# Twelve activation turns of the second pass by DMA transposes instead of TensorE, with the lists of ScalarE and VectorE reordered

## The reference, cut to what matters

```python
# first branch, "d" is a long convolution of the context, worked out apart
y  = layernorm(layernorm(x));  y = silu(y @ W1a + b1a) @ W1b + b1b + ...   # first pass
y  = y * d                                                                 # gate
z  = layernorm(y) * g2 + be2;  z = silu(z @ W2a + b2a) @ W2b + b2b + y     # second pass
x  = x + tanh(g_xattn) * z
# second branch: experts on heads of 32 numbers
h  = layernorm(x) @ Wm + bm                    # "third norm" and "head products"
t  = h.reshape(-1, 32);  w = softmax(t @ expert_emb);  top-2 of 16 experts
x  = x + tanh(g_ffn) * (sum of two experts of t, weighted) @ Wo + ...
```

## Time and profile before

| | |
|---|---|
| runs | 808.10, 813.09, 814.97 us; median 813.09 us |
| span of the profiled execution | 807.5 us |
| PE busy | 774.8 us (96%) |
| ACT busy | 670.3 us (83%) |
| DVE busy | 531.4 us (66%) |
| POOL busy | 496.0 us (61%) |
| second pass | about 180 to 300 us from the start |
| experts | from about 300 us to the end |

### The profile page before, as it was taken

One profiled execution on the slowest core, in us unless ns is written; L12 is line 12 of the kernel. 1 busy time (PEld: TensorE's weight loads), 2 busy tenths in 40 slices (PEclk: granted clock), 3 DMA queues, 4 the chain that ended last, 5 costly groups with the idle time before them and its releaser, 6 DMA issues.

```text
span 807.5 us, 23892 instructions
## 1 busy us (share of the span) xinstructions
PE 774.8 (96%) x9972; PEld 380.7 (47%) x9972; DVE 531.4 (66%) x988; ACT 670.3 (83%) x840; POOL 496.0 (61%) x389
## 2 busy tenths in 40 slices
PE   9999788889999998998999999999999999999997
PEld 4667455646676664333334434434434433434433
DVE  5999854557688985684665664764764764664445
ACT  4465854445869878799999999999999999999995
POOL 1374332027753542585787787787787787787674
PEclk9999999979999999999999999999999999999999
DMA  8990699941133316655465554555555555465552
GB/s 291 219 244 28 135 187 191 198 107 36 50 86 89 89 44 166 156 143 149 145 158 151 166 157 147 159 170 146 157 159 151 165 159 155 148 171 158 149 154 67
DMA packets 85971, 117.06 MB, mean 145 GB/s; under 512 B 13123, under 2 KB 65475, under 8 KB 85764
## 3 DMA queue, kind: packets, MB, share of 16 engines
q1 hardware_dynamic: 85864, 115.55, 55.2%
HBM read 101.28 MB, written 6.94 MB: 134 GB/s over the span
## 4 chain that ended last, share of the span: by engine, by line
PE 71%; DVE 10%; ACT 7%; SPq 5%; issue 3%; DMA 2%; POOL 2%; POOLq 0%; DVEq 0%; ACTq 0%
PE PB L792 26%; PE PA L780 18%; PE PT L780 9%; PE PA L581 5%; SPq L345 4%; PE PB L598 3%; PE PB L814 2%; PE PA L535 2%; DMA RA<-wpd 2%; DVE WK L897 2%; DVE SM L914 1%; ACT WK L1458 1%; PE PT L673 1%; ACT WK L1438 1%; ACT WK L1435 1%
## 5 line engine op out<-in xcount | busy, mean ns | idle before, releaser
L1677 POOL TENSOR_TENSOR WK<-WK 128x512 f32<-128x512 f32 x238 | 320.3, 1346 | 112.3 <-DVE WK L1333 102.2
L1582 ACT ACTIVATE WK<-PA 128x1024 f32<-128x1024 f32 x349 | 360.1, 1140 | 10.8 <-PE PA L780 10.3
L792 PE MATMUL PB<-WK,EW 128*32 128x512 f32 x2040 | 264.7, 594 | 0.4 <-DVE WK L1333 0.4
L780 PE MATMUL PA<-RA,EW 98*32 98x512 f16 x2800 | 201.6, 380 | 0.5 <-ACT WK L1582 0.5
L1582 ACT ACTIVATE WK<-PT 128x1024 f32<-128x1024 f32 x163 | 187.1, 1148 | 2.0 <-PE PT L780 1.7
L1610 POOL TENSOR_TENSOR WK<-WK 128x512 f16<-128x512 f32 x64 | 79.5, 1255 | 129.9 <-ACT WK L1438 128.6
L780 PEld LDWEIGHTS PA<-RA,EW 98*32 98x32 f16 x2800 | 68.1, 95 | 154.9 <-issue 80.4
L780 PE MATMUL PT<-RA,EW 98*32 98x512 f16 (+1 forms) x1312 | 99.6, 379 | 4.8 <-ACT WK L1582 3.4
L792 PEld LDWEIGHTS PB<-WK,EW 128*32 128x32 f32 x2040 | 62.4, 111 | 52.3 <-DVE WK L1333 0.9
L1333 DVE SCALAR_TENSOR_TENSOR WK<-PB,CV,W2h 128x512 f32<-128x512 f32 x64 | 48.1, 751 | 49.1 <-PE PB L792 49.1
L1333 DVE SCALAR_TENSOR_TENSOR WK<-PB,CV,W2l 128x512 f32<-128x512 f32 x63 | 47.3, 751 | 44.3 <-PE PB L792 44.3
(11 more groups left out here) (220 smaller groups left out, 1086.8 us busy)
## 6 DMA issues: line engine op xcount, KB each, us to landing
RA<-wpd SPq DMA_DIRECT2D x128, 134.1 KB, 5.8
W1h<-wtd SPq DMA_DIRECT2D x128, 128.0 KB, 2.7
DC<-wtd SPq DMA_DIRECT2D x128, 128.0 KB, 2.8
W2h<-wtd SPq DMA_DIRECT2D x128, 128.0 KB, 2.7
W2l<-wtd SPq DMA_DIRECT2D x128, 128.0 KB, 2.7
WK<-in_x SPq DMA_DIRECT2D x15, 512.0 KB, 4.0
RA<-DC SPq DMA_DIRECT2D x96, 64.0 KB, 2.0
out<-WK SPq DMA_DIRECT2D x16, 256.0 KB, 2.8
```

Source lines behind the costliest of these rows:

```text
L780: m = pe.matmul(pre(k)[32 * j:32 * j + 32, w * q:w * q + w], EW1[0:98, 128 * e + 32 * j:128 * e + 32 * j + 32], TS[0:98, h, t0:t0 + w], st ...
L792: m = pe.matmul(o[32 * q:32 * q + 32, :], EW2[:, 32 * e:32 * e + 32], hb[:, 512 * q:512 * q + 512], start=True, stop=True)
L1582: ac.activation(HB[n % NH][:, 1024 * p:1024 * p + 1024], pre(k)[:, :], ACT.Gelu, scale=1.0 / (SC * SC)).then_inc(a_gelu, 1)
L1677: po_.tensor_tensor(AC[g], AC[g], PR[m % 3], ALU.add).then_inc(g_ac, 1)
```

## The change

For b from 2 to 7 the gated turn, and for b from 0 to 5 the third turn, are made by transfers instead of TensorE: twelve of sixteen turns of the second pass. The turns of the gated blocks 0 and 1 and of the third blocks 6 and 7 stay on TensorE. ScalarE now makes the high part ahead of the turn, as one copy of 128x1024 (`split_rows`), VectorE the low part (`gated_lo`, `third_lo`), both into a float16 tensor of 128x2048 (`GN`, or `TN3`, which is the weight tensor W1h, free by then); SP issues one DMA transpose of it (`turn_rows`), 512 KB, into `XT[t % 2]`. `layer1` and `heads` on TensorE wait for the transfer instead of for VectorE.

```diff
@@ SP
+            def turn_rows(t, rows, count, done):
+                sp.wait_ge(count, done)
+                sp.wait_ge(*xt_freed(t - 2))
+                both = WK[:, 3072 + 1024 * (t % 2):4096 + 1024 * (t % 2)].bitcast(F16)
+                sp.dma_start_transpose(both.rearrange("p (j n) -> p j n", n=128), rows[:, :]).then_inc(s_xt[t % 2], 16)
             for s in range(NB):
                 if s >= 1 and s + 1 < NB:
                     sp.wait_ge(v_out, 8 + s)
                     load_x(1, s + 1)
+                    turn_rows(turn2(s + 1), GN, v_g2, s)
                 if s >= 2:
                     spread_heads(s - 2)
+                if 1 <= s < NB - 1:
+                    turn_rows(turn3(s - 1), TN3, v_g3, s)
@@ PE, step s
-                if s >= 2:
-                    third_turn(s - 2)
...
-                if s + 1 < NB:
-                    gated_turn(s + 1)
+                if s == 0:
+                    gated_turn(1)
@@ PE, layer1 (heads alike, for b < 6)
-                pe.wait_ge(v_lo, 2 * t + 2)
+                if t > turn2(1):
+                    pe.wait_ge(*turned(t))
+                else:
+                    pe.wait_ge(v_lo, 2 * t + 2)
@@ DVE
+            def gated_lo(b):
+                ve.wait_ge(a_g2, b - 1)
+                ve.tensor_tensor(by_halves(GN[:, 1024:2048]), XN.rearrange("p (t k c) -> p t k c", k=2, c=128),
+                                 by_halves(GN[:, 0:1024]), ALU.subtract).then_inc(v_g2, 1)
...
@@ DVE, step s
-                if s >= 1:
-                    turn_lo(turn2(s))
-                    if s + 1 < NB:
-                        gated_stats(s + 1)
-                        norm_shift(norm2(s + 1))
+                if s == 1:
+                    turn_lo(turn2(1))
+                if 1 <= s < NB - 1:
+                    norm_shift(norm2(s + 1))
+                second_sum(s)
                 for i in ROUTE0.get(s, ()):
                     route(0, i)
                 if s >= 1:
                     second_out(s - 1)
-                if s >= 2:
-                    turn_lo(turn3(s - 2))
-                if s >= 1:
                     third_stats(s - 1)
-                second_sum(s)
+                    if s + 1 < NB:
+                        gated_lo(s + 1)
+                    norm_shift(norm3(s - 1))
                 if s >= 3:
                     less_max(s - 3, PB[:, 0:512])
-                if s == 7:
-                    norm_shift(norm3(6))
                 if s >= 2:
                     heads_lo(s - 2)
-                if 1 <= s < 7:
-                    norm_shift(norm3(s - 1))
+                if s + 2 < NB:
+                    gated_stats(s + 2)
+                if 1 <= s < NB - 1:
+                    third_lo(s - 1)
@@ ACT, step s
-                if s >= 2:
-                    third_norm(s - 2)
...
                 if s + 1 < NB:
                     gated_norm(s + 1)
-                if s >= 2:
-                    turn(turn3(s - 2))
+                    if s >= 1:
+                        gated_hi(s + 1)
                 layer1(8 + s, C_B2A)
+                if s == 0:
+                    turn(turn2(1))
+                else:
+                    third_norm(s - 1)
+                    if s < NB - 1:
+                        third_hi(s - 1)
                 if s >= 2:
                     heads(s - 2)
-                if s + 1 < NB:
-                    turn(turn2(s + 1))
-                else:
-                    third_norm(6)
```

More of the change, by code:

```diff
@@ L63, in turn3, with by_tensor, by_transfer @@
     return norm3(b)
+def by_tensor(t):
+    return (*range(NB), turn2(0), turn2(1), 22, 23).index(t)
+def by_transfer(t):
+    ts = [turn2(b) for b in range(2, NB)] + [turn3(b) for b in range(6)]
+    return sorted(u for u in ts if u % 2 == t % 2).index(t)
 def norm2(b):
@@ L92, in transposer_uses @@
     out = [("conv", 0, 0), ("conv", 0, 1)]
[L93 to L96, removed]
+    out += [("turn", turn2(b), k) for b in range(2) for k in range(2)]
+    out += [("head", b, g) for b in range(6) for g in range(2)]
     out += [("wt", 0, 0), ("turn", 22, 0), ("turn", 22, 1), ("head", 6, 0), ("head", 6, 1),
@@ L197, in flamingo_kernel @@
         po_at = {u: i for i, u in enumerate(po_list)}
-        late_turns = [turn2(b) for b in range(3, NB)]
+        GN = WK[:, 5120:6144].bitcast(F16)
+        TN3 = W1["h"]
         def pt(kind, i, k):
@@ L260, in flamingo_kernel @@
         s_tl = [sem(f"s_tl{b}") for b in range(NB)]
+        s_xt = [sem(f"s_xt{i}") for i in range(2)]
         s_zx = [sem(f"s_zx{u}") for u in range(4)]
         s_out = [sem(f"s_out{u}") for u in range(2)]
-        s_wt = [sem(f"s_wt{b}") for b in range(NB)]
+        s_wt = [sem(f"s_wt{i}") for i in range(2)]
         l_wb = [sem(f"l_wb{i}") for i in range(4)]
@@ L541, in turn @@
                 for k in range(2):
[L542 to L545, removed]
+                    if t >= NB:
                         bank = take_pt("turn", t, k)
@@ L1462, in gated_norm, with split_rows, gated_hi, third_hi @@
             def gated_norm(b):
-                ac.wait_ge(*((p_turn, 2 * turn2(b - 1) + 2) if b else (v_wo, 1)))
-                normed(norm2(b), XR[:, 1024 * b:1024 * b + 1024], XN, a_n2)
+                if b == 0:
+                    ac.wait_ge(v_wo, 1)
+                elif b < 3:
+                    ac.wait_ge(p_turn, 2 * by_tensor(turn2(b - 1)) + 2)
+                else:
+                    ac.wait_ge(v_g2, b - 2)
+                normed(norm2(b), XR[:, 1024 * b:1024 * b + 1024], XN, a_n2)
+            def split_rows(x, to, done):
+                ac.activation(to.rearrange("p (k t c) -> p t k c", k=2, c=128), x.rearrange("p (t k c) -> p t k c", k=2, c=128),
+                              ACT.Copy).then_inc(done, 1)
+            def gated_hi(b):
+                if b == 2:
+                    ac.wait_ge(v_eb, 1)
+                else:
+                    ac.wait_ge(*turned(turn2(b - 1)))
+                ac.wait_ge(a_n2, b + 1)
+                split_rows(XN, GN[:, 0:1024], a_g2)
+            def third_hi(b):
+                if b:
+                    ac.wait_ge(*turned(turn3(b - 1)))
+                ac.wait_ge(a_n3, b + 1)
+                split_rows(WSP[:, 1024 * b:1024 * b + 1024], TN3[:, 0:1024], a_g3)
             def third_norm(b):
```

30 lines of the change are left out of this document (21 added, 9 removed).

## The result

The changed kernel takes 834.78 us (median of 4 runs, 831.06 to 838.12), the kernel before beside it 812.1 us (4 runs, 808.1 to 814.97). The ratio is 1.0316, 95% interval 1.0278 to 1.0353: slower by 3.2%, where 1.4% was forecast. The sign is right, and the size is off by more than half.

What follows compares the result with a forecast made beforehand. A loop through ACT, DVE and POOL, 16.8 to 18.1 us a step, was to bind, not PE. First lag +4.6, four loops +6.2, last term +1.35, experts -0.7: +11.5, giving 824.5 us, range 811 to 856.

Steps and rivals of the forecast that it cites:

- The signs named for it: Second pass: steps of 16.8 to 18 us, ACT without a gap from SiLUs to heads, PE idle 2 to 3 us.
- The links in ACT's own time: ACT's part of the loop: gated norm and split 3.15 us, eight SiLUs 4.56, third norm and split 3.15, heads to `heads_lo` 2.2.
- T: Time for a DMA transpose to land, taken as 5 us, with 2 and 12.6 as ends.
- the last term: From block 4's `heads_lo` to the end of the last heads fed by a transfer: 15.35 us against 14.0, +1.35.
- the links through POOL and DVE's small instructions: In each loop: 3.5 us from `heads_lo` to the gated norm; third norm's shift about 0.2 us late, 0.8 with routing.
- The first lag: Stretch up to the first `heads_lo`: 3.15 us third norm and split, 1.2 gated split and `second_sum`, 0.25 shift; +4.6.
- PE's idle time: PE in the second pass: idle stretches of 2 to 3 us a step, ahead of the head products or layer one.
- The -0.7: Experts' start on ACT: block 6's third norm no longer stands ahead of it, part of its 2.08 us counts, -0.7.
- Slow transposes: Rival: landing above 6.5 us sets the loop; 837 us at 8 us landing, 879 in an extreme form; chance 0.2.
- an unchanged chain: Rival: the chain through ACT, DVE and POOL stays 15.5 to 16 us, 809 to 817 us; chance 0.17.
- PE as the pace: Rival: the chain falls below 14.14 us and steps shrink to PE's work, 11.7 us less, 801; chance 0.10.
- the likeliest case: The forecast itself: landing below 6.5 us, chain at 16.6 to 18 us, 817 to 833 us; chance 0.53.

Runs made afterwards that it cites:

- run 4: Changed kernel with each transpose moving only the high halves, 128x1024, so products use stale low halves: 835.0 us, ratio 1.0319 to the kernel before.
- run 5: Changed kernel with ScalarE's heads of block s-2 put ahead of the third norm and split of block s-1: 826.67 us, ratio 1.02 to the kernel before.
- run 8: Kernel before with only the six gated turns made by DMA, third turns on PE, lists otherwise as before: 812.12 us, ratio 1.0037.
- run 1: Changed kernel with `third_lo` moved on VectorE behind the next step's norm shift: 831.26 us, ratio 1.027 to the kernel before.
- run 2: Changed kernel with `gated_lo` moved on VectorE behind the third norm's shift: 831.16 us, ratio 1.0274 to the kernel before.
- run 3: Changed kernel with both `third_lo` and `gated_lo` moved later on VectorE: 829.93 us, ratio 1.0249 to the kernel before.
- run 9: Kernel of run 5 plus ten matmuls of ones on PE ahead of its wait for the third transposes: 820.11 us, ratio 1.0133 to the kernel before.
- run 6: Kernel of run 5 with `third_lo` and `gated_lo` also moved later on VectorE: 825.8 us, ratio 1.0182 to the kernel before.
- run 7: Kernel of run 6 with SP issuing the third transpose ahead of `spread_heads`: 815.29 us, ratio 1.0071 to the kernel before.
- run 10: Kernel of run 7 with VectorE's `less_max` ahead of the third norm's shift: 816.4 us, ratio 1.0083 to the kernel before.
- run 11: Kernel of run 8 with VectorE's `less_max` ahead of the third norm's statistics: 816.05 us, ratio 1.0086 to the kernel before.

## Why the prediction was right in sign and wrong in size

- **What binds.** Right. PE's 96% was no argument for a gain. The time is set by the loop from `heads_lo` to `heads_lo` (runs 4 and 5), and 10.4 us of work taken off PE bought nothing, also where only half was taken (run 8). The signs named for it came in part: steps of 19.2 to 19.8 us where 16.8 to 18 stood, and ACT does have a gap ahead of the third norm, 1.1 to 2.4 us, where none was to be.
- **The links in ACT's own time.** Right to 0.15 us: gated norm and split 3.14 us (3.15), eight SiLUs 4.71 to the end of the last one (4.56, which was taken to the start of the next instruction), third norm and split 3.13 (3.15), heads to `heads_lo` 2.11 (2.2). So were the copy of 128x1024 (1.06) and the subtraction (1.22).
- **T, and the last term.** Right: 4.3 and 5.1 us against 5, beside 5.0 us for the 512 KB load of x in the same kernel, and 15.4 against 15.35; there is luck in the last, since these head products happened to run at full clock. Half the size still took 3.2 to 3.5 (run 4).
- **The failed step: the links through POOL and DVE's small instructions.** The prediction wrote "`third_lo` (1.2) now lies inside it while POOL's 1.01 runs" and took 3.5; measured 4.21, since the 1.01 is 1.91 beside `third_lo`. It wrote "POOL needs 1.2 more, its power 1.0, the shift 0.2", and took 0.2 us of waiting; measured 1.90 in step 3, of which 0.84 is the `layer1_lo` pair beside `gated_lo` and 0.95 the shift beside the next pair. In steps 4 and 6 it is the power that meets `gated_lo` (1.91 us, waits of 2.44 and 2.28), in step 5 only the shift is late (1.07). That is about 2.2 us a step above the forecast, 8.6 over four. The first lag has two such third norms, late by 1.89 and 1.91 us where 0.25 was taken in all, which is enough for its missing 3.1; that is arithmetic and was not tried by itself. Runs 1 to 3 moved the excess about with the subtractions; both moves together took 1.6 us of the lag and 3.2 of the four loops away, somewhat under half of the 11.7 in question. What stays in run 3 is read from its rows and was not tried: the shift's 0.95, and in steps 4 and 6 the new order on DVE.
- **What I could have read.** The kernel before has this in its own trace, where it cost little. POOL's and DVE's timelines of before:
```profile
233.50 1.97 POOL L1604 TENSOR_TENSOR SM<-SM 128x4 f32<-128x4 f32 x1
```
```profile
206.29 1.11 DVE L940 SCALAR_TENSOR_TENSOR SM<-SM 128x4 f32<-128x4 f32 x1 [3.12 <-POOL SM L1604]
...
233.34 1.27 DVE L1111 SCALAR_TENSOR_TENSOR WK<-XR,SM,WK 128x1024 f32<-128x1024 f32 x1
```
 The power of 1.97 us runs beside DVE's L1111, which reads two tiles of SBUF, and ends 0.86 after it; the shift of 1.11 beside a `layer1_lo` pair. I took the mode of a group, 1.01 and 0.2, for the price. And the change made more of such meetings: the split's subtractions read PSUM and SBUF before (L897 <-PT,WK), and now SBUF twice (L935 <-DC,W1h; L930 <-WK). Beside the old form (1.27 us from 207.32 on) a `layer1_lo` pair took 2.26 us from 206.23 on, no surcharge.
 The Trainium skill, page "SBUF — State Buffer", section "Who interferes with whom", has it as a rule: the port pair that the two engines share is an exclusive lock, and a DVE instruction with two SBUF inputs contends with a GpSimd instruction that reads SBUF. One with at most one SBUF input does not, outside the modes in which DVE uses both ports, of which the page says that whoever issues first holds the pair for the whole instruction. The trace agrees with the first part from both sides: 1.91 us for 1.01, where POOL came second, and 1.11 for 0.16, where DVE did. It also has a row with one input that is held up: the small L967 of the statistics, 0.17 us elsewhere, takes 1.67 us at 207.35, beside a `gate` of POOL, and both end at 209.0. Weighed in the prediction, the rule would have asked for a price for two or three such meetings a step; at the 0.9 us each of the rows that is the missing 2 us.
- **PE's idle time.** Forecast 2 to 3 us a step, measured 3.9 on average (3.0 to 5.3). That the granted clock of the matmuls behind it falls from the 2.4 to the 1.2 GHz level (0.50 from 238.57 on), in three of five cases, was not forecast. In the changed kernel this lies beside the longer loop; by run 9 it is worth 8.8 us of M once that loop is gone.
- **The end.** The -0.7 did not come. The experts' part took 1.2 us more. The store of the first weights landed in 4.58 us instead of 2.3, and DVE waits 6.6 us at L1372 for what is read back from it; runs 5 to 11 have 2.3 again, runs 1 to 4 have 3.5 to 4.2. Why it is slow in those is open. Whether it makes the 1.2 us is not shown either: in runs 1 and 2 DVE waits 5.4 us there, and the experts' part is 508.4 and 508.3 us, near the 508.1 of before.
- **The rivals.** Slow transposes are excluded by 4.3 to 5.1 us of landing and by run 4, an unchanged chain and PE as the pace by loops of 19.2 us and more and by PE's idle time. The range of 811 to 856 held the time; the likeliest case's own, 817 to 833, did not.

## What to carry to other kernels

Ask of a piece taken off the busiest engine which list it is put into, and write out the loop that this list closes across the engines; here a norm and a split of 3.1 us came to stand between two links of a loop, and the heads put ahead of it on ACT and the transpose ahead of `spread_heads` on SP regained 2.5 of the 3.2% (two subtractions moved on DVE brought nothing when only the heads had been put ahead). Price a small instruction of POOL or DVE by what runs on the other one beside it, and look whether an edit turns a DVE operand from PSUM into SBUF. Idle time of PE ahead of its products can count twice when they stand in the loop, once as a wait and once as a lower clock behind it; here matmuls for nothing, put into that wait, paid for themselves.

## What the runs showed of the hardware

- A DMA transpose of 128x2048 float16 from SBUF to SBUF lands in 4.3 to 5.1 us in the changed kernel (medians; up to 5.5 over all runs), with half the size in 3.2 to 3.5; its row on SP's queue lasts 1.6 to 3.7 us, where a 64 KB copy has mostly 0.63 (5.07 to 6.04 for eight).
- POOL's power on 128x4 takes 1.01 us, and 1.91 to 1.97 beside a DVE instruction that reads two tiles of SBUF; two of its subtractions of 128x512 take 2.31 us, and 3.15 to 3.33 beside one; a DVE shift of 128x4 takes 0.16 us, and 1.10 to 1.11 beside a POOL pair that started just ahead of it.
- After 4.6 us of idle the head products took 5.3 us at a granted clock of 0.50, with a pair of matmuls 1.04 instead of 0.59; after ten matmuls of ones and 1.6 us of idle they took 2.8 at 1.00. Behind shorter idle times both occurred: slow behind 2.30 us (run 5), at full clock behind 3.21 us (changed kernel).
